# Attention steps written out for every image, routing positions two steps later, their running sum on VectorE, rows normalised once and copied

## What is computed

```python
# attention, after x = layernorm(tokens)
content_score = einsum('bshd,bthd->bhst', q + u_bias, k)
pos_score = rel_shift(einsum('bshd,thd->bhst', q + v_bias, p))
attn = softmax((content_score + pos_score) / sqrt(D), axis=-1)
ctx = einsum('bhst,bthd->bshd', attn, v).reshape(B, S, D)
t = t + ctx @ Wout + bout
# experts, after x = layernorm(t)
gate_logits = x @ Wg + bg
top_w, top_i = top_k(gate_logits, 2)
top_w = softmax(top_w)
out = sum over e of w_dense[:, e] * (gelu(x @ W1[e] + b1[e]) @ W2[e] + b2[e])
```

## Time and profile before

| | us |
|---|---|
| Time, median of 3 runs | 4112.44 (4105.55 to 4118.47) |
| Time of the profiled execution | 4110.17 |
| Its span, first to last instruction | 4107.7 |
| Attention, from the first copy of `wide_ps` to the last | 1311 to 3443 |
| PE, DVE, ACT, POOL busy over the span | 3243.4, 2720.2, 2203.8, 745.2 |

### The profile page before, as it was taken

The page is one execution under the profiler, slowest core; times in us unless marked ns, Lnnn a source line. Parts: engine busy times, 40 slices in busy tenths (PEclk is TensorE's granted clock), DMA queues, the critical chain, the costliest instruction groups (busy, mean ns, idle before and its releaser), DMA issues. The chain is left out here.

```text
span 4107.7 us, 80297 instructions
## 1 busy us (share of the span) xinstructions
PE 3243.4 (79%) x29652; PEld 2491.6 (61%) x29652; DVE 2720.2 (66%) x5162; ACT 2203.8 (54%) x3568; POOL 745.2 (18%) x869
## 2 busy tenths in 40 slices
PE   4789888987565888787887787878877885699993
PEld 2555655665453666666666665667666764587772
DVE  4877787776443767666766676667666764477773
ACT  2545555554453656555655565556655653477770
POOL 1000000000111020212021202120212112466660
PEclk9999999998777988888998898888888987799995
DMA  2544554454587999888988898889888983477768
GB/s 54 162 121 155 177 158 125 159 172 141 213 306 245 364 332 321 296 298 303 326 318 281 302 332 301 293 292 326 318 283 302 336 302 134 165 238 238 244 207 328
DMA packets 291011, 1023.87 MB, mean 249 GB/s; under 512 B 51620, under 2 KB 57520, under 8 KB 281574
## 3 DMA queue, kind: packets, MB, share of 16 engines
q1 hardware_dynamic: 273382, 985.62, 69.7%
q0 software_dynamic: 17280, 33.87, 2.3%
HBM read 486.25 MB, written 489.85 MB: 238 GB/s over the span
## 5 line engine op out<-in xcount | busy, mean ns | idle before, releaser
L1089 DVE CUSTOM_DVE_ANT_0 att_skewed<-att_score_ps,att_skewed 128x1024 f32<-128x1024 f32 x512 | 625.5, 1222 | 325.5 <-issue 303.9
L951 ACT ACTIVATE att_skewed<-att_skewed,att_neg_max 128x1024 f32<-128x1024 f32 x512 | 588.8, 1150 | 369.1 <-DVE att_neg_max L1089 332.9
L942 ACT ACTIVATE att_rows<-att_wide_ps 128x1152 f32<-128x1152 f32 x512 | 573.8, 1121 | 371.0 <-PE att_wide_ps L1171 282.9
L1097 DVE COPY att_turned<-att_turn_ps 128x1024 f32<-128x1024 f32 x512 | 625.4, 1222 | 148.1 <-remote 109.0
L1207 PE MATMUL att_turn_ps<-att_ident,att_skewed 128*128 128x128 f32 x4096 | 598.1, 293 | 119.1 <-ACT att_skewed L951 93.9
L1207 PEld LDWEIGHTS att_turn_ps<-att_ident,att_skewed 128*128 128x128 f32 x4096 | 499.5, 150 | 290.4 <-ACT att_skewed L951 218.6
L1171 PE MATMUL att_wide_ps<-att_ps,att_qs 98*128 98x128 f32 (+3 forms) x1920 | 455.7, 360 | 44.0 <-ACT att_rows L942 19.0
L1217 PE MATMUL att_tail_ps<-att_turned,att_vals 128*32 128x128 f32 x8192 | 320.1, 288 | 125.9 <-issue 124.2
L1199 PE MATMUL att_score_ps<-att_ks,att_qs 96*128 96x512 f32 x1024 | 385.3, 460 | 15.4 <-DVE att_neg_max L1089 14.1
L906 POOL DMA_INDIRECT expert_rows<-att_expert_rows,att_place x256 | 247.1, 965 | 787.8 <-DVE att_place L1047 702.0
L1171 PEld LDWEIGHTS att_wide_ps<-att_ps,att_qs 98*128 98x128 f32 x1920 | 324.3, 209 | 104.4 <-issue 49.0
(11 more groups left out here) (256 smaller groups left out, 5301.9 us busy)
## 6 DMA issues: line engine op xcount, KB each, us to landing
skewed_rows<-att_rows SPq DMA_DIRECT2D x512, 576.0 KB
att_skewed<-skewed_rows SPq DMA_DIRECT2D x512, 512.0 KB, 6.2
expert_rows<-conv_pad SPq DMA_DIRECT2D x144, 520.0 KB, 10.9
exp_weights<-split_weights SPq DMA_DIRECT2D x71, 1028.0 KB
att_qs<-queries SPq DMA_DIRECT2D x192, 128.0 KB
att_ks<-keys SPq DMA_DIRECT2D x192, 128.0 KB
exp_rows<-expert_rows SPq DMA_DIRECT2D x71, 260.0 KB
sum_part<-expert_parts SPq DMA_DIRECT2D x32, 512.0 KB, 8.6
```

Source lines behind the costliest of these rows:

```text
L942: act.activation(rows[s % ROWS][:], wide_ps[:, 0:WIDE], ACT.Copy).then_inc(wide_read, 1)
L951: act.activation(skewed[r % RING][:], skewed[r % RING][:], ACT.Exp, bias=neg_max[:, k:k + 1], scale=-1.0, accum_out=sums[:, k:k + 1]).then ...
L1089: dve.tensor_tensor_reduce(skewed[r % RING][:], score_ps[:], skewed[r % RING][:], -SCALE, 3.0e38, ALU.add, ALU.min, neg_max[:, k:k + 1]).t ...
L1097: dve.tensor_copy(turned[r % (2 * HEADS)][:], turn_ps[:]).then_inc(turn_read, 1)
```

## The change

Four things are changed, all in `attention_phase`.

1. The loop over pairs of images is gone: the slots of all 16 images are written out on TensorE, VectorE, ScalarE and SyncE.
2. The counting product moves from slot 25 to slot 27, and part 4 of `gating` from slot 26 to 28; parts 0 to 3 stay in slots 22 to 25. The last image's routing takes 30 slots instead of 28.
3. VectorE forms the sum of `chosen` over all tiles before each tile, by three additions of shifted copies (by one, two and four tiles) in `padded`, `by_two` and `by_four`, whose zero borders GpSimd sets once. TensorE then needs one product with `ones`, of 72 columns, instead of eight.
4. GpSimd normalises only into `expert_rows[0]` (8 instructions) and then copies the whole to `expert_rows[1]` in one. TensorE waits for `normed >= 2m + 1`.

```diff
-ROUTE_AT, STATS_AT, OFFSET_AT, NORMED_AT, GATES_AT, POWER_AT, PLACES_AT, ROUTE_END = 9, 10, 15, 18, 22, 24, 25, 28
+ROUTE_AT, STATS_AT, OFFSET_AT, NORMED_AT, POWER_AT, PLACES_AT, ROUTE_END = 9, 10, 15, 18, 24, 27, 30
+GATES_AT = (22, 23, 24, 25, 28)
...
-            image(0, 0)
-            with eng.Fori(0, (NB - 2) // 2) as pair:
-                image(2 * pair + 1, 1)
-                image(2 * pair + 2, 0)
-            image(NB - 1, 1)
+            for n in range(NB):
+                image(n, n % 2)
...
-                for k in range(2):
-                    for t in range(TT):
-                        ins = pool.tensor_scalar(expert_rows[k][:, t, 0:C], z[:, t * P:(t + 1) * P], rstd[:, t:t + 1],
-                                                 offset[:, t:t + 1], ALU.mult, ALU.add)
-                    if k == 0:
-                        ins.then_inc(normed, 1)
+                for t in range(TT):
+                    ins = pool.tensor_scalar(expert_rows[0][:, t, 0:C], z[:, t * P:(t + 1) * P], rstd[:, t:t + 1],
+                                             offset[:, t:t + 1], ALU.mult, ALU.add)
                 ins.then_inc(normed, 1)
+                pool.wait_ge(normed, 2 * m + 1)
+                pool.tensor_copy(expert_rows[1][:, :, 0:C], expert_rows[0][:, :, 0:C]).then_inc(normed, 1)
...
-                k = r - GATES_AT
+                k = GATES_AT.index(r)
...
-                    dve.tensor_scalar(flat(chosen[:]), rank[:], 1.5, None, ALU.is_lt).then_inc(chosen_ready, 1)
+                    gate_chain.step(dve.tensor_scalar(flat(chosen), rank[:], 1.5, None, ALU.is_lt))
+                    gate_chain.step(dve.tensor_tensor(by_two[:, 2:, :], padded[:, 1:, :], padded[:, 0:1 + TT, :], ALU.add))
+                    gate_chain.step(dve.tensor_tensor(by_four[:, 4:, :], by_two[:, 2:, :], by_two[:, 0:1 + TT, :], ALU.add))
+                    dve.tensor_tensor(so_far[:], by_four[:, 4:, :], by_four[:, 0:1 + TT, :], ALU.add).then_inc(chosen_ready, 1)
...
-                    pe.wait_ge(normed, 2 * m + 2)
+                    pe.wait_ge(normed, 2 * m + 1)
...
-                    pe.matmul(spare[:, 0:TT * E], before[:], flat(chosen[:]), start=True, stop=False, skip_group_check=True)
-                    for t in range(TT):
-                        pe.matmul(spare[:, (t + 1) * E:(TT + 1) * E], ones[:], chosen[:, t:t + 1, :].to_broadcast([P, TT - t, E]),
-                                  start=False, stop=False, skip_group_check=True)
+                    pe.matmul(spare[:, 0:TT * E], before[:], flat(chosen), start=True, stop=False, skip_group_check=True)
+                    pe.matmul(spare[:, 0:(TT + 1) * E], ones[:], flat(so_far[:]), start=False, stop=False, skip_group_check=True)
```

More of the change, by code:

```diff
@@ L885, in _ @@
             pool.memset(ones[:], 1.0).then_inc(consts_set, 1)
+            for border in (padded[:, 0:2, :], by_two[:, 0:2, :], by_four[:, 0:4, :]):
+                pool.memset(border, 0.0).then_inc(consts_set, 1)
             pool.iota(token_int[:], [[P, TT]], base=0, channel_multiplier=1).then_inc(consts_set, 1)
```

10 lines of the change are left out of this document (6 added, 4 removed).

## The result

| kernel | time, us (median, lowest to highest) | against before (95% interval) |
|---|---|---|
| before | 4114.88 (4105.55 to 4118.47, 4 runs) | 1 |
| changed | 4013.09 (4006.68 to 4016.72, 4 runs) | 0.9759 (0.974 to 0.9778) |
| forecast | 4006, range 3905 to 4080 | |

The change saves some 100 us, 2.4%, and the forecast is 7 us off. The profiled execution took 4016.72 us, 93.45 less than the one of before; the sum had said 106.8. The total is right, but it is made of other parts than the sum's.

A forecast was written before the change was run, and what follows sets the result against it. TensorE's products and the DMA queues were both taken as near their limit. 15 images x (0.5 + 5.0) = 82.5, plus 18.6, plus 5.7, is 106.8 us off the median 4112.44: 4006, range 3905 to 4080.

The forecast's parts named there:

- The loop's ends: Last slot of images 2, 4, 6, 8, 10 and 12: without the jump, 3.1 us each given back, 18.6 us.
- The copy on GpSimd: GpSimd's copy to the second half of the expert rows: 1.7 us, hidden ahead of the scatter, so no cost.
- the three additions: VectorE's three additions of 72 columns for the count: 0.25 us each with their waits, 0.75 us.
- `normed`: Slots 17 and 18, TensorE's wait for GpSimd's normalising: gain of 0.5 us an image, between 0 and 4.8.
- The count: Slots 24 to 28, wait for `chosen` gone and fewer passes: gain of 5.0 us an image, between 3.0 and 6.6.
- The hold: Engines crawling or standing during the scatter: moves with the scatter's end, length unchanged, 0 us, within 1 us an image.
- the slower rival: At the scatter: dense run caught from the start, 22.8 us instead of 12.3, so 158 us more, 4163; chance 0.06.
- the sign of being wrong: At the scatter: a crawl that is gone or starts with the scatter would show the forecast wrong; no size given.
- The rival that a dense run alone crawls: Slot 30: only a run of 64 small passes crawls, so most of 12.3 us goes, 165 more, 3841; chance 0.07.
- The DMA rival: Slots 17, 18 and 24 to 28: queues are no bound, both waits give all, 195 us, 3917; chance 0.2.
- the end: Routing after the last image, covered by nothing: 3.4 us from normalising and 2.3 from the count, together 5.7 us.

The follow-up runs named there:

- scatter_4_times_4: Changed kernel with the scatter's 16 indirect DMAs in four bunches of four, each issued after a dense run of value products: 3788.67 us, ratio 0.9175.

## Why the prediction was right, and where it was not

**Right:** the waits for `normed` and `chosen` are gone, VectorE waits for read-backs instead, and even images are no longer than odd ones, though an image takes 129.5 us where 127 to 128 had been named. The DMA share of image 3 is 0.97 to 1.03 from slot 8 to 28, as foreseen. The loop's ends are worth 20.3 us by run (18.6 forecast). The copy on GpSimd is hidden (1.04 us, estimated 1.7), and the three additions take 0.76 us (0.75).

**`normed`: 0.5 us an image forecast, 2.1 measured.** The value came from the lower end because a landing had released VectorE after the transposes. The step that failed was to take this landing as fixed in time and as what the slot waits for. With the wait gone, VectorE's operation starts 60.1 us into image 3 (1740.67 less 1680.6) instead of 61.0. And the landing was not the end of the slot's chain. ScalarE's next operation waited for TensorE before, whose transposes and 64 value passes stood behind the wait for `normed`, and waits for VectorE now (the row of the kernel before, then that of the changed kernel):

```profile
1751.89 0.49 ACT L921 ACTIVATE att_z<-att_wide_ps 128x384 f32<-128x384 f32 x1 [2.19 <-PE att_wide_ps L1171]
...
1741.93 1.15 ACT L952 ACTIVATE att_skewed<-att_skewed,att_neg_max 128x1024 f32<-128x1024 f32 x1 [2.72 <-DVE att_neg_max L1093]
```

So the copy that follows comes 2.8 us behind VectorE's start instead of 5.1, with TensorE at a granted clock of 1.00 over the two slots instead of 0.86. Of the 4.2 us that slots 17 and 18 lose when the wait is put back, half is made up for in slots 19 to 28.

**The count: 5.0 forecast, 3.0 left by difference, with the longer hold in it.** Without the 2.0 us of the hold (below) the count gave 5.0 by the runs, and 4.4 by the profiled executions (4.5 an image, less 2.1 for `normed`, plus 2.0). So the size was about right. The reason was right in part. The 5.0 was the idle share of the DMA queues, and that idle did go (a share of 1.03 and 0.97 where it had been 0.76 and 0.84), but slots 24 to 28 of image 3 gave 3.3 us and not 5, since they now move 7.3 MB instead of 6.7, by the rows' GB/s. And the two edits don't add up: in slots 24 to 28 the place is worth 1.7 us with VectorE's sum there, and the sum nothing once the place has moved.

**The hold: 0 forecast, 2.0 us an image lost** (slots 29 to 31, from 25.3 to 27.3). The reason given was that its end goes with the scatter's end. That held. Its beginning does not: it goes with the first dense run that meets the scatter, and the change moved the scatter to 3 us ahead of one. This was the slower rival's mechanism, "caught from the start", which had put 10.5 us an image on it. VectorE's standstill indeed runs from 4.4 us (the end of its last copy, 1788.75) to 22.9 us behind the first DMA. It is also the sign of being wrong that the prediction had named, "a crawl that ... starts with the scatter". The trace of the kernel before had this case in it already. The prediction set the mechanism aside because "VectorE stood still in image 8 with no such run on it", and that is a misreading. In image 8 GpSimd paused after the first DMA, and the dense run met the second:

```profile
2472.50 0.97 POOL L906 DMA_INDIRECT expert_rows<-att_expert_rows,att_place  x1 [6.86 <-issue]
...
2473.04 1.88 PE L1217 MATMUL att_tail_ps<-att_turned,att_vals 128*32 128x128 f32 x45
2475.28 0.44 PE L1217 MATMUL att_tail_ps<-att_turned,att_vals 128*32 128x128 f32 x5 [0.37 <-issue]
```

It stopped after 45 passes, 2.4 us behind the start of the second DMA, and the operation of VectorE that the earlier trace rows shows with 19.60 us of idle time is the one that waits for this run. Slots 29 to 31 of that image took 30.8 us, or 27.7 without the jump's 3.1, which is what every image pays now.

But the stretch ahead of the crawl was not as free before as the earlier trace rows let it seem: in slot 29 TensorE's transposes had ended 5.5 us behind the scatter's start and were known to VectorE 1.7 us late, and that slot took 6.5 us. Against the kernels with four bunches, which have no hold (slots 29 to 31 in 9.7 us with the positions in slot 25, in 10.4 in slot 27), it cost 15.6 us before and costs 16.9 now: some 1.3 of the 2.0 are the hold, 0.7 the routing's work that moved there. The rival's 10.5 us came out so small for two reasons: the hold of before cost more than the 12.3 us that were counted, and the one of now begins 4.4 us behind the first DMA and costs 16.9, not 22.8. The rival that a dense run alone crawls was wrong on the place it named: the crawl did not go, since the run now meets the scatter's beginning.

**The DMA rival** (the queues are no bound, 3917) was wrong on the time and on its reason: with the loads at an eighth an image gains 3.2 us, 2.8 of them in slots 17 to 23, so the transfers did cost time there.

**The rest.** In the two profiled executions images 0 to 14 give 82.1 us: 18.6 from the jumps and 63.5, or 4.5 for each of the 14 that have routing in them, where 5.5 had been forecast. Image 15 and what follows until the last scatter give 18.0 instead of 11.2. There the hold of image 14's scatter falls behind the last copy in the changed kernel and ahead of it before; that this is the reason is not shown. The expert and convolution stages differ by some 7 us the other way between these two executions, and have no part in the change. So a gain that was put too low (`normed`, the end) and a loss that was put at nothing (the hold) cancelled; the 7 us are partly luck. The upper end of the prediction's own range, by its terms, is 4069 and not 4065 (4112.4 less 45, 18.6 and 5.7, plus 26).

The larger matter was in sight and was not taken up: "this is the dearest place" stood over the scatter, and its cost was then carried along as a constant. It was worth 224 us, more than twice the change.

## What to carry to other kernels

When a change moves a long burst of DMAs of GpSimd, look at what stands in the slots where it lands: here its price was set by the work that it met, and a delay that removed a wait lengthened a stall by about as much. Two edits on one stretch need not add up: here the shorter count was worth nothing once it stood where TensorE had time for it. And before a wait is tuned away, price the longest standstill of the period and try to cut what causes it into pieces: a landing or a clock behind a wait moves with the wait and is no reason to write it off. And where the trace of before has an odd case in it (here the scatter with a pause), read it before a rival is set aside: it may be the experiment already made.

## What the hardware showed unexpectedly

Sixteen indirect DMAs from GpSimd, issued 1.26 us apart, slow TensorE to a crawl and keep VectorE and ScalarE standing for 18.5 us, whether they carry 1.07 MB or 0.11 MB. Two ways in were seen. Where a run of small products (64 passes) meets DMAs in flight (3.1 us behind the first of sixteen), the hold starts within it and ends 2.3 to 2.8 us behind the end of the last issue. Without such a run, what TensorE had finished 5.5 to 6.6 us behind the first was known to the others 1.7, 3.3 and 4.8 us late, while the DMAs went on or had just ended. Four in a row (5 us) that no dense run met held nothing. Where a dense run met few DMAs, the hold was short: 2.4 us of VectorE's time for DMAs in pairs, and at one place of the run `scatter_4_times_4` (2338.0), where a dense run met the third of three DMAs behind the pause told of below, it stopped after 38 passes and took 2.7 us instead of 2.0. In the changed kernel's image 3 the trace's semaphore events show that TensorE goes on slowly and its updates don't arrive: that of a product that ended at 1796.4 us arrives at 1807.2, one of 1800.8 at 1807.3, while those of other engines before it are prompt. This is why the others stand, released by nothing that the profile can name. What inside the chip holds the updates back is open.

The Trainium skill (SBUF — State Buffer, section "SBUF: two separate sides") says that a DMA cannot be slowed by a compute operation and vice versa, and that TensorE and ScalarE never wait on anyone at their SBUF ports. The runs don't contradict this of the ports, since a tenth of the bytes changed nothing; but whoever reads it as leave to place GpSimd's DMAs anywhere loses, in this kernel, 224 us.

In two of the sixteen scatters of either kernel GpSimd pauses for 6.5 to 7.9 us after the first or second DMA, for no releaser. Counted over the attention's 256 indirect DMAs the pauses stand ahead of the 114th and the 227th, so 113 apart, and they stand there in the runs with changed bunches, bytes and normalising too. It isn't explained. In the changed kernel the dense run of slot 30 of image 8 falls into the pause, behind a single DMA that had ended 2.0 us before, and passes freely (3.7 us for the slot instead of 20.8). Nothing is won by it: the fifteen DMAs that follow meet the next dense run, and slot 2 of image 9 takes 18.4 us instead of 3.8.
